# Layer 0 of a graph network: two count tables summed by GpSimd's accumulating loads in place of VectorE additions

## The reference, cut to what matters

```python
agg = segment_sum(h[src], dst, num_segments=N)
deg = segment_sum(ones(src.shape[0]), dst, num_segments=N)
mean_agg = agg / maximum(deg, 1.0)[:, None]
out = mean_agg @ Wl + bl + h @ Wr
...
out = (out - out.mean(axis=0)) * rsqrt(out.var(axis=0) + EPS) * gamma + beta
h = relu(out)
```

## Time and profile before

| | us |
|---|---|
| median of 3 runs | 3320.3 (3317.73 to 3321.78) |
| the profiled execution, its own time | 3317.77 |
| its span | 3316.0 |
| mean granted TensorE clock | 0.86 |
| PE busy | 2340.6 (71%) |
| DVE busy | 1357.6 (41%) |
| POOL busy | 888.8 (27%) |
| ACT busy | 410.1 (12%) |

### The profile page before, as it was taken

The page is one execution under the profiler, slowest core; times in us unless marked ns, Lnnn a source line. Parts: engine busy times, 40 slices in busy tenths (PEclk is TensorE's granted clock), DMA queues, the critical chain, the costliest instruction groups (busy, mean ns, idle before and its releaser), DMA issues.

```text
span 3316.0 us, 41358 instructions
## 1 busy us (share of the span) xinstructions
PE 2340.6 (71%) x14511; PEld 1816.7 (55%) x14511; DVE 1357.6 (41%) x2835; ACT 410.1 (12%) x822; POOL 888.8 (27%) x642
## 2 busy tenths in 40 slices
PE   1131100001389899998998887899989995999997
PEld 1121100000266676776776346688878884888886
DVE  6698877777143211111113763212311577111111
ACT  0010000000000420000400222200020000223222
POOL 2588888888300000000001130000000000333332
PEclk9965555555799999999998887999999997999999
DMA  9833333332676059973035000144424433566665
GB/s 352 277 39 38 32 38 37 33 38 7 222 296 275 23 165 262 250 226 99 0 129 174 1 0 0 52 148 150 146 62 147 146 115 121 155 195 183 184 189 140
DMA packets 289019, 426.59 MB, mean 129 GB/s; under 512 B 166226, under 2 KB 224519, under 8 KB 288887
## 3 DMA queue, kind: packets, MB, share of 16 engines
q1 hardware_dynamic: 105335, 297.03, 27.3%
q10 hardware_dynamic: 109696, 106.77, 10.3%
q0 software_dynamic: 73936, 22.14, 7.9%
HBM read 307.61 MB, written 100.96 MB: 123 GB/s over the span
## 4 chain that ended last, share of the span: by engine, by line
PE 58%; POOL 16%; DVE 7%; issue 6%; DMA 3%; ACT 2%; DVEq 0%; ACTq 0%; POOLq 0%; SPq 0%
PE ps L1558 14%; POOL odd_counts L505 8%; POOL at_counts L505 8%; PE ps L1782 8%; PE ps L1783 7%; PE ps L1860 7%; PE ps L1851 7%; PE ps L1573 4%; PE ps L1502 4%; DMA xrows<-odd_counts 3%; PE ps L1733 1%; PE ps L1632 1%; PE ps L1760 1%; ACT harena L827 1%; DVE harena L1153 1%
## 5 line engine op out<-in xcount | busy, mean ns | idle before, releaser
L1558 PE MATMUL ps<-ring,harena 128*128 128x320 f16 x4000 | 546.6, 299 | 50.0 <-DVE ring L1057 48.1
L1782 PE MATMUL ps<-harena,ring 128*128 128x257 f16 x2500 | 556.3, 274 | 3.7 <-DVE harena L1240 2.7
L1783 PE MATMUL ps<-harena,ring 128*128 128x256 f16 x2500 | 555.9, 273 | 0.0
L1558 PEld LDWEIGHTS ps<-ring,harena 128*128 128x128 f16 x4000 | 391.7, 98 | 205.2 <-issue 52.6
L1525 PE MATMUL ps<-harena 128*128 128x25 f16 x416 | 20.1, 184 | 623.9 <-DVE harena L982 582.4
L970 DVE SCALAR_TENSOR_TENSOR late<-ring,ps 128x1024 f16<-128x1024 f32 x312 | 378.9, 1274 | 107.7 <-POOLq L531 107.7
L505 POOL DMA_INDIRECT at_counts<-ring x224 | 346.4, 1546 | 151.9 <-issue 66.7
L1525 PEld LDWEIGHTS ps<-harena 128*128 128x128 f16 x416 | 15.3, 105 | 630.0 <-DVE harena L982 587.1
L505 POOL DMA_INDIRECT odd_counts<-ring x192 | 299.9, 1562 | 58.5 <-issue 57.3
L1782 PEld LDWEIGHTS ps<-harena,ring 128*128 128x128 f16 x2500 | 243.1, 97 | 43.4 <-DVE harena L1284 3.8
L1783 PEld LDWEIGHTS ps<-harena,ring 128*128 128x128 f16 x2500 | 243.4, 97 | 32.7
(11 more groups left out here) (339 smaller groups left out, 2667.9 us busy)
## 6 DMA issues: line engine op xcount, KB each, us to landing
ring<-at_counts SPq DMA_DIRECT2D x150, 800.0 KB, 4.4
ring<-L_ffn_W SPq DMA_DIRECT2D x64, 1024.0 KB, 5.4
ring<-ad_counts SPq DMA_DIRECT2D x50, 800.0 KB, 4.3
ring<-key_rows SPq DMA_DIRECT2D x52, 512.0 KB, 3.7
at_counts<-tarena ACTq DMA_DIRECT2D x5, 4000.0 KB, 37.9
odd_counts<-tarena ACTq DMA_DIRECT2D x5, 4000.0 KB, 38.4
xrows<-odd_counts SPq DMA_DIRECT2D x25, 800.0 KB, 9.6
at_counts<-ring ACTq DMA_DIRECT2D x25, 800.0 KB, 8.5
```

Of the source, the lines that this page charges most:

```text
L1558: ins = M(ps[:, 2 * f + h, 0:HB], part[:, t, (2 * k + f) * P:(2 * k + f + 1) * P], chunk[q][:, s, h * HB:(h + 1) * HB], start=(t == 0 and ...
L1782: M(ps[:, i, 0:F + 1], lhs, hh[:, t, 0:F + 1], start=(t == 0), stop=False)
L1783: ins = M(ps[:, i, 0:F], lhs, hl[:, t, :], start=False, stop=(t == T - 1))
```

## The change

The `odd_counts` chunk is no longer loaded into a staging buffer and added by DVE. POOL issues it as an accumulating DMA that adds to the slot of the ring while it lands. The semaphores `sum_in[0]` and `sum_in[1]` (named `sums_landed`, by the parity of n) take the place of `tables_summed` and `odd_in`. POOL waits for the `at_counts` chunk and for the accumulating load of chunk n - 2, so at most two of them are in flight. ACT and PE wait on `sum_in`. DVE has no part in the sum, and its block loop is a loop again; PE's block loop of layer 0 is written out, since the semaphore alternates.

```diff
@@ SP
-                if n >= 2:
-                    sp.wait_ge(tables_summed, n - 1)
-                sp.dma_start(odd_chunk[n % 2], odd[:, b, part]).then_inc(odd_in[n % 2], 16)
@@ POOL, after the last scattered additions
+            for n in range(NB * NB):
+                b, q = n // NB, n % NB
+                pool.wait_ge(chunk_in[q], 16 * (b + 1))
+                if n >= 2:
+                    pool.wait_ge(sum_in[n % 2], 16 * (n // 2))
+                pool.dma_start(chunk_flat[q], odd[:, b, q * BT * BC:(q + 1) * BT * BC], accum_op=ALU.add, max_dma_last_dim=3200).then_inc(sum_in[n % 2], 16)
+
             pool.wait_ge(ent[0][5], NB * 4 + 1)
             pool.dma_start(wr2, w["L0_gnn_Wr1"].rearrange("(d p) f -> p d f", p=P)).then_inc(wr1_in, 16)
@@ ACT
-                wait(tables_summed, n + 1)
+                wait(sum_in[n % 2], 16 * (n // 2 + 1))
@@ DVE
-                def sum_tables(b, q):
-
-                    n = b * NB + q
-                    dve.wait_ge(chunk_in[q], 16 * (b + 1))
-                    dve.wait_ge(odd_in[n % 2], 16 * (n // 2 + 1))
-                    V.tensor_tensor(chunk_flat[q], chunk_flat[q], odd_chunk[n % 2], ALU.add).then_inc(tables_summed, 1)
-
-                if l == 0:
-                    for q in range(NB):
-                        sum_tables(0, q)
-                    for b in range(NB - 1):
-                        for q in range(3):
-                            sum_tables(b + 1, q)
-                        aggregated(b, HB)
-                        for q in range(3, NB):
-                            sum_tables(b + 1, q)
-                else:
-                    with o.loop(NB - 1, 2 * nfo) as b:
-                        aggregated(b, HB)
+                with o.loop(NB - 1, 2 * nfo) as b:
+                    aggregated(b, HB)
@@ PE
                     if l == 0:
-                        pe.wait_ge(tables_summed, b * NB + (q + 1))
+                        m = b * NB + q
+                        pe.wait_ge(sum_in[m % 2], 16 * (m // 2 + 1))
...
-            with pe.Fori(0, NB) as b:
+            for b in range(NB):
                 aggregate(0, b, 0, F)
                 mean_products(0, b, 2, 4)
```

More of the change, by code:

```diff
@@ L156, in build @@
         turned_rows16 = xrows[:, :, :].rearrange("p t c -> p (t c)").bitcast(fp16)
-        odd_chunk = [turned_rows16[:, k * BT * BC:(k + 1) * BT * BC] for k in range(2)]
         turned = [runs(turned_rows16[:, s * BT * BC:(s + 1) * BT * BC], a=BT) for s in range(TURNS)]
@@ L285, in build @@
         krow_in = [sem(f"krow_in{s}") for s in range(LOOK)]
-        compared, idx_ready, even_added, odd_added, groups_landed, tables_summed = map(sem, ("compared", "idx_ready", "even_groups_added", "odd_groups_added", "groups_landed", "tables_summed"))
-        odd_in, sum_out = ([sem(f"{name}{k}") for k in range(2)] for name in ("odd_counts_in", "sums_stored"))
+        compared, idx_ready, even_added, odd_added, groups_landed = map(sem, ("compared", "idx_ready", "even_groups_added", "odd_groups_added", "groups_landed"))
+        sum_in, sum_out = ([sem(f"{name}{k}") for k in range(2)] for name in ("sums_landed", "sums_stored"))
         chunk_in = [sem(f"chunk_in{q}") for q in range(NB)]
```

## The result

| | before | after |
|---|---|---|
| median of 13 runs each, us | 3320.3 (3317.31 to 3322.08) | 3311.8 (3308.59 to 3315.01) |
| ratio to before, 95% interval | | 0.9974 [0.9966, 0.9983] |
| the profiled execution, its own time | 3317.77 | 3311.77 |
| its span | 3316.0 | 3310.0 |
| layer 0: first chunk load to the last block's weight products | 866.41 to 1078.29: 211.9 | 867.98 to 1075.05: 207.1 |

The kernel became faster by 0.26%, 8.5 us, where 12 us slower was forecast. The time is that of rival 1 (3312) and inside the range.

A forecast was written before the change was run, and what follows sets the result against it. The prediction took the DMA engines to bound layer 0 after the change: 968.7 + 3 + 25 x 4.7 ends it at 1089.2, 11.9 us later, which added to the 3320.3 median gives 3332 us; range 3303 to 3387.

The forecast's parts named there:

- rival 1: Accumulating loads in layer 0 cost only a second read, c 3.9 us or less: 8.1 us earlier, 3312; chance 0.26.
- c: DMA engine time of one accumulating odd_counts load of 819,200 bytes in layer 0, taken as 4.7 us against 1.95 plain.
- the DMA line: Layer 0's end if DMA work bounds it: 968.7 + 25c, plus 3 us; passes the old 1077.3 at c = 4.2.
- 92 ns per KB: Price of accumulating data, from POOL's 1 KB scatter rows (136 ns) less a 2-byte scattered addition (44 ns); gave c near 4.6.
- The 44 ns of a scattered element: Engine time of a scattered 2-byte addition, taken as a latency that packets of other queues can fill when engines are full.
- The rule named beside the sum: A reduction in the DMA engines needs two source reads, measured ratio 1.93; by it c would be 3.8 us, the median 3309.
- The waits before the weight products go to five of 1.0: PE's waits before layer 0's weight products fall from 22.4 us over five blocks to five times 1.0.
- The first sum comes at 880.3: Block 0's first summed chunk lands at 880.3 against 876.99, with 9.6 us for POOL's issue and the landing.
- both lines: The two bounds on layer 0's end: DMA work, 1089.2 at c = 4.7, and PE's own work, 1056.5, 20.8 us earlier.
- Chunks 8 to 9 us apart with PE waiting for most: Expected profile sign from 868 to 1075 us: PE waits for odd_counts DMAs before most chunks, c between 4.5 and 5.4.
- Two in flight is no limit: Two accumulating loads in flight limit layer 0 only if one takes over 17 us from issue to landing; then 9.6.
- Everything behind layer 0 moves as a whole: What follows layer 0 keeps its length, so layer 0's 11.9 us delay is added unchanged to the whole time.

## Why the prediction was wrong

**The failed step is the size of c,** "I take 4.7, close to the 4.6". Measured by itself it is 3.98 us. With it the DMA line gives 968.7 + 3 + 25 x 3.98 = 1071.2, 6.1 us earlier than before, and 3314 for the median, where 3311.8 was measured. The break-even was 4.2, between the two values, so this term alone turned the sign. The closeness of 3314 is in part luck: in the profiled executions the last matmul of layer 0 ended only 3.2 us earlier (1074.15 against 1077.3), and a gain behind layer 0, which the sum put at nothing, made up for it.

**Why c was off.** 92 ns per KB came as a difference of two bursts of scattered rows, and the earlier trace rows, of 256 and 4752 packets. Measured on the operation it is 3.98 x 16 = 63.7 engine-us for 256 pieces, 249 ns each; less the 9 ns for a piece, 240 ns for 3.1 KB, 77 ns per KB. That is two plain passes of 39. The 44 ns of a scattered element stand against 9 ns for a piece in a full queue, so most of it may be time that a full queue hides, as the prediction guessed; part of the 92 may be of that kind too, which the prediction didn't ask. No run separates this. A row "measured on this operation" was taken over the lower bound, though it was another form of it (indirect, 1 KB, two in 6 us).

**The rule named beside the sum was right.** The Trainium skill, Collectives: The Full Stack, section "The bandwidth ceiling: the fold count and why AG ≠ RS ≠ AR", says that the addition costs no time of its own and needs two source reads. The page measured it on collectives between cores. This case's ratio agrees: 210 against 420 GB/s, 3.98 against 1.99 us, 2.0 where the page has 1.93. The sum by it, 3309, was nearer than the forecast.

Point by point:
- *The waits before the weight products go to five of 1.0*: 0.92 each. Right.
- *The first sum comes at 880.3*: 884.70. Two parts: the first load was issued 1.6 us later, and the accumulating load took 12.2 us to land, not 9.6 with its issue. Beside the same `at_counts` loads but without the addition it took 8.4 us, so 3.8 us of the 12.2 are the second pass. This term was missing: c was counted as work of the engines, not as latency of the first chunk.
- *The DMA line*: right as a mechanism. The DMA share was 1.05, the pace 7.61 us a chunk against 3.9 + 3.98 = 7.9 worked out, 7.49 with three in flight. The last store, which waits for the last sum, was issued at 1066.5; with 5.5 for PE's chunk that is 1072.
- *PE's last matmul ended at 1074.15*, 2 us behind that. PE had lost 14.3 us early (9.7 in block 0, 4.6 in block 2), through waits of 7.6 us and about as much of slow matmuls after them, and then ran blocks 3 and 4 without a wait, 37.0 us each. So both lines were within some 2 us of each other at the end: the engines set the first three blocks and PE the last two.
- *Chunks 8 to 9 us apart with PE waiting for most*: three waits besides the first. Wrong with c. q0's share gives 0.544 x 150 / (15.91 / 0.819) = 4.2 us, and 4.0 once the share of 1.05 is scaled to 1.
- *Two in flight is no limit*: right, shown by three in flight. It would be one at a latency near 17 us; the median went from 9.6 to 14.5. By the measured pace of 7.61 us the bound is 15.2, so the margin is thin.
- *POOL's issue of 1.46 us*: 1.19. *`wr` behind the 25*: it isn't in the waits. Both were rightly counted for nothing.

**Where the 8.5 us are.** In the profiled pair, 6.0 us apart, the stage starts 1.6 us later and is 4.8 us shorter, and what follows takes 2.8 us less. "Everything behind layer 0 moves as a whole" didn't hold. From the start of the last weight products to the end of the span, the six kernels in which POOL loads `odd_counts` into the ring took 2232.7 to 2235.5 us, and the five in which DVE makes all the sums 2235.2 to 2241.2, on average 3.9 us more. The medians say the same: without the addition and with one sum ahead the stage is as long (191.7 and 190.8), but the medians are 3292.7 and 3299.3. So some 3 to 4 of the 8.5 us may come from behind layer 0. Why is open; no run was made on this.

**What the change was worth.** In the stage it buys 20 us for PE by freeing it from DVE's order and pays 15 back to the second read. Rival 1's price was the right one. None of the cases asked whether the gain could be had without the cost; it can, by the order alone.

## What to carry to other kernels

An accumulating DMA saves an engine an addition but took the DMA engines twice the time of a plain one: count its bytes twice, and ask for the share of the DMA engines in the busiest stretch first. Where the waits name an engine that stands in an order with other work ahead, first try the order: here, as few sums as possible ahead of a step that is due, and as many between two such steps in every round. A price from a short burst of small packets didn't scale to long rows here; when the sign hangs on it, bound it by the plain rate times the passes.

## What the runs showed of the hardware that was not expected

- A direct accumulating load of 819,200 bytes runs at 210 GB/s and a plain one at 420, in fp16 and fp32 alike, while the profile counts its bytes once. A view can thus show 311 GB/s with the engines full.
- A further piece of a row costs 9 ns of an engine when the engines are full; one of 2 bytes in a sparse burst 44.
- GpSimd takes 1.19 us to issue such a load in 256 pieces, 1.55 in 1024, and 0.57 for a plain one.
- With two in flight and full engines, issue to landing had a median of 14.5 us (18.1 with three; 9.7 with one, where the share was 0.91), while one with nothing else running took 7.4. From two to three only the latency grew.
- After PE waited 4.01 us, 40 matmuls took 7.28 us in place of 5.5, and after 2.77 us 7.26, but after 0.77 us 5.61. The granted clock of that stretch, 986 to 1026, was 0.96, against 1.00 in the same window of the kernel without the addition, where PE didn't wait. A short wait cost PE up to 1.8 us more than itself. Its length alone doesn't decide: with the smaller pieces, 40 matmuls took 5.61 us after a wait of 2.30 and 7.28 after one of 2.04.
